# An id match in a DLRM look-up: one VectorE compare with row numbers in PSUM, or eight with all operands in SBUF

## What is computed

```python
e = jnp.stack([tbl_0[ids[:, 0]], ..., tbl_25[ids[:, 25]]], axis=1)
combined = jnp.concatenate([dense[:, None, :], e], axis=1)        # (2048, 27, 128)
inter = jnp.einsum('bnd,bmd->bnm', combined, combined)            # upper triangle is kept
h = jnp.concatenate([dense, inter_flat, dense], axis=1)
h = jnp.maximum(h @ W_top1 + b_top1, 0.0)
h = jnp.maximum(h @ W_top2 + b_top2, 0.0)
y = h @ W_top3
```

## Time and profile before

| | |
|---|---|
| median of 3 runs | 382.88 us (381.33 to 383.34) |
| profiled execution | 384.91 us |
| its span (first to last instruction) | 382.8 us |
| mean granted TensorE clock | 0.991 of full speed |
| POOL, 256 gathers | 248.8 us busy, 75.0 us of issue between them |
| DVE, 80 matches | 181.7 us busy |
| PE | 341.9 us busy |

### The profile page before, as it was taken

How to read it: one execution, slowest core, us unless ns; L and a number is a source line. 1 busy time by engine, 2 the same in 40 slices (tenths; PEclk the granted TensorE clock), 3 DMA queues, 4 the chain that set the end, 5 groups by cost and what they waited for, 6 DMA issues and landing times.

```text
span 382.8 us, 13108 instructions
## 1 busy us (share of the span) xinstructions
PE 341.9 (89%) x6048; PEld 304.2 (79%) x6048; DVE 193.2 (50%) x94; ACT 125.5 (33%) x211; POOL 252.1 (66%) x267
## 2 busy tenths in 40 slices
PE   0788878984999999999999999999999999999995
PEld 0687767883898898898988898889988898977763
DVE  2899996565424396228833495238742595100000
ACT  2235433332132341334322342323322333343122
POOL 3777887777777777777777777777777777500200
PEclk9999999999799999999999999999999999999999
DMA  8975698254322537225632536234622533420400
GB/s 205 222 210 166 170 301 250 58 195 126 126 80 58 193 82 200 58 80 177 149 119 58 194 92 190 58 120 140 187 79 58 193 89 86 144 73 27 154 13 0
DMA packets 30868, 49.57 MB, mean 129 GB/s; under 512 B 17499, under 2 KB 17635, under 8 KB 30686
## 3 DMA queue, kind: packets, MB, share of 16 engines
q1 hardware_dynamic: 22350, 31.68, 27.0%
q0 software_dynamic: 8320, 16.92, 16.8%
q10 hardware_dynamic: 144, 0.13, 0.1%
HBM read 38.21 MB, written 10.49 MB: 127 GB/s over the span
## 4 chain that ended last, share of the span: by engine, by line
PE 72%; POOL 14%; issue 6%; DMA 4%; DVE 2%; ACT 1%; DVEq 0%
PE look_ps L309 28%; POOL rows L290 14%; PE mid_ps L339 13%; PE layer_ps L356 11%; PE layer_ps L365 7%; PE mid_ps L321 7%; PE layer_ps L353 4%; DMA rows<-in_table,index 3%; DVE match L463 2%; PE layer_ps L372 2%; DMA index<-in_index 1%; ACT hidden L528 0%; ACT hidden L534 0%; ACT turned L501 0%; ACT turned L512 0%
## 5 line engine op out<-in xcount | busy, mean ns | idle before, releaser
L290 POOL DMA_INDIRECT rows<-in_table,index x256 | 248.8, 972 | 82.3 <-issue 75.0
L463 DVE TENSOR_TENSOR match<-look_ids,row_number_ps 125x2048 fp32r<-125x2048 int32 x80 | 181.7, 2286 | 132.2 <-PE look_ps L309 122.3
L309 PE MATMUL look_ps<-match,table_high 125*128 125x256 f32 x640 | 165.7, 296 | 20.2 <-DVE table_low L471 18.1
L309 PE MATMUL look_ps<-match,table_low 125*128 125x256 f32 x640 | 159.4, 286 | 0.1
L309 PEld LDWEIGHTS look_ps<-match,table_high 125*128 125x128 f32 x640 | 124.8, 195 | 25.0 <-issue 16.0
L309 PEld LDWEIGHTS look_ps<-match,table_low 125*128 125x128 f32 x640 | 125.1, 195 | 0.0
L339 PEld LDWEIGHTS mid_ps<-turned 128*32 128x32 f32 x4096 | 45.3, 109 | 19.1 <-issue 15.3
L339 PE MATMUL mid_ps<-turned 128*32 128x27 f32 x4096 | 54.4, 195 | 5.5 <-issue 1.7
L501 ACT COPY turned<-look_ps 128x512 f32<-128x512 f32 x40 | 31.9, 798 | 73.5 <-PE look_ps L309 72.2
L508 ACT COPY turned<-mid_ps 128x512 f32<-128x512 f32 x64 | 42.8, 672 | 19.7 <-PE mid_ps L321 19.5
L321 PE MATMUL mid_ps<-identity,rows 128*128 128x128 f32 x256 | 40.6, 283 | 9.4 <-DMA rows<-in_table,index 8.5
(11 more groups left out here) (21 smaller groups left out, 44.8 us busy)
## 6 DMA issues: line engine op xcount, KB each, us to landing
look_ids<-in_look_rows SPq DMA_DIRECT2D x40, 256.0 KB, 4.4
scratch<-grams SPq DMA_DIRECT2D x8, 864.0 KB, 4.4
rows<-in_table,index POOLq DMA_INDIRECT x256
scratch<-grams SPq DMA_DIRECT2D x8, 416.0 KB, 5.2
pairs<-scratch SPq DMA_DIRECT2D x92, 29.2 KB
grams<-in_table SPq DMA_DIRECT2D x4, 448.0 KB
pairs<-in_table SPq DMA_DIRECT2D x3, 448.0 KB
hidden<-in_table SPq DMA_DIRECT2D x3, 448.0 KB
```

Source lines behind the costliest of these rows:

```text
L290: pool.indirect_dma_start(out=rows[j % 2][:, at, :], out_offset=None, in_=tables[GATHERED[at]], in_offset=bass.IndirectOffsetOnAxis(ap=ind ...
L309: last = nc.tensor.matmul(look_ps[pair % 2][:, r % 2, :], part[0:table_rows, r, c, :], match[number % 2][0:table_rows, c, :], start=(c == ...
L463: nc.vector.tensor_tensor(match[number % 2][0:table_rows], look_ids[b][0:table_rows, r % 2].unsqueeze(1).broadcast_to(shape), row_number_p ...
```

## The change

The row numbers no longer go to PSUM but, as fp32, to a tile `row_number_f` in SBUF. The two rows of ids of a pair are cast to fp32 in place, once a pair, and DVE waits for its own cast. A match is then eight instructions, one per part c, each comparing the 256 ids of every partition with one row number per partition, `row_number_f[:, c:c+1]`. All operands of a match now lie in SBUF. The semaphore `match_ready` rises with the eighth compare, as it rose with the one before. The bank of PSUM that is freed is used for nothing.

```diff
+        row_number_f = sbuf("row_number_f", [P, PARTS])
...
-        row_number_ps = psum("row_number_ps", [P, PARTS])
-
...
+        ids_cast = sem("ids_cast")
...
+        def cast_number(g, q):
+            return pair_number(g, q)
...
                 b = pair % ID_SLOTS
+                ids_f = look_ids[b][0:table_rows].bitcast(fp32)
                 if r % 2 == 0:
                     dve.wait_ge(look_ids_in[b], 16 * (pair // ID_SLOTS + 1))
+                    nc.vector.tensor_copy(ids_f, look_ids[b][0:table_rows]).then_inc(ids_cast, 1)
+                    dve.wait_ge(ids_cast, cast_number(g, r // 2) + 1)
 
                 after(dve, look_done, number - 1)
-                shape = [table_rows, PARTS, N]
-                nc.vector.tensor_tensor(
-                    match[number % 2][0:table_rows],
-                    look_ids[b][0:table_rows, r % 2].unsqueeze(1).broadcast_to(shape),
-                    row_number_ps[0:table_rows].unsqueeze(2).broadcast_to(shape),
-                    ALU.is_equal).then_inc(match_ready, 1)
+                for c in range(PARTS):
+                    last = nc.vector.tensor_scalar(match[number % 2][0:table_rows, c, :], ids_f[:, r % 2, :],
+                                                   row_number_f[0:table_rows, c:c + 1], None, ALU.is_equal)
+                last.then_inc(match_ready, 1)
...
-            nc.vector.tensor_copy(row_number_ps[:], row_number[:]).then_inc(row_numbers_copied, 1)
+            nc.vector.tensor_copy(row_number_f[:], row_number[:]).then_inc(row_numbers_copied, 1)
```

## The result

The changed kernel is slower by 2.3%: 391.19 us median (388.16 to 393.56, 4 runs) against 383.11 us, a ratio of 1.0229 (95% interval 1.0172 to 1.0287). Run again in a later series it gave 392.94 us, ratio 1.0222 (1.0168 to 1.0277). The forecast was 456 us, with a range of 388 to 505. Medians and ranges are of all runs; the ratios leave out a run that is over 1.5% above the fastest of its kernel. The profiled execution took 388.16 us, the fastest of the four, with a span of 386.1 us; the one before was the slowest of its four (384.91 us, span 382.8). So the two profiles differ by 3.3 us, less than half of what the medians do.

What follows compares the result with a forecast made beforehand. It took POOL's gathers to bound the kernel up to 96 us, then PE, with POOL about 7 us behind. Gather holds of 77 us plus 3 for casts, less 7, gave +73 on 382.8: 456 us, range 388 to 505.

Steps and rivals of the forecast that it cites:

- What bounds the kernel: Whole kernel: gathers on POOL set the path up to 96.35 us, then PE, a group in some 42.4 us.
- The slack of 7 us: POOL at the run's end: it can lose about 7 us; any loss beyond comes out one for one.
- Step 1: Match on DVE: the new compare reads ids and row number from SBUF, so it can hold gathers; 80 matches of eight.
- the split's case: DVE instruction with two SBUF operands: a gather's index read waits for its end, then the gather needs 0.82 us.
- Step 2: Length of the eight compares on DVE: 1.58 us together, between 0.5 and 2.65, and 0.28 us for one.
- Step 3: Cast of the ids on DVE: 0.42 us, 40 times, lying in DVE's idle time except in the opening.
- Step 5: DVE's match: 1.8 us with half a cast against 2.2 before, taking off at most 0.7 us of PE's waiting.
- The last of the signs named in the prediction: DVE's compares: if POOL holds DVE instead, compares of up to 0.8 us stand among short ones.
- Step 6: POOL's gathers: each burst of eight holds one for 0.96 us, 77 us; with casts 80, less slack, +73 us.
- The let-in case: POOL's gathers: let in between compares, waiting 0.14 us on average; +10 us, 393 us in all; chance 0.27.
- the slow DVE: DVE's matches: no gather held, but one element a cycle, 2.65 us a match; 410 us in all; chance 0.07.
- The wholly stopped case: POOL's gathers: compares also stop descriptor writing, so gathers barely advance in bursts; up to +136, 519 us; chance 0.12.

Runs made afterwards that it cites:

- 32 gathers: Gathers stop after two tiles, 32 of 256, and later turns reread those rows: 368.33 us on the kernel before, 370.75 us on the changed kernel.
- the tail: The changed kernel with 27 more DVE instructions after its last match, compares and copies of 128, 256 and 512 elements: 387.21 us in its one run.

## Why the prediction was wrong

It was right that the change is slower, and wrong in size and in the engine that pays: +73 us on POOL was forecast, +8 us on DVE was measured. That 391 us lies inside the range of 388 to 505 is luck: its low end stood for POOL losing time to compares shorter than 0.28 us, and the compares took 0.34 us and POOL lost nothing.

**What bounds the kernel.** Right: with 32 gathers the kernel before falls from 382 to 368 us, and with gathers that are held (the second tensor in SBUF) the loss goes through to the end. The slack of 7 us fits the latter as well, the lower clock left aside: POOL loses 105 us and the kernel 99.

**Step 1, "the split's case, not the old match's".** This is the step that failed. It counted the row number as a second SBUF operand of the same kind as the split's. The run with the row number in PSUM shows that its place changes nothing, so it does not count as a second operand. The run with a second tensor in SBUF is the split's case: it held a gather in every match, for 1.4 us, where the changed kernel's bursts of eight hold one for 0.1 us or not at all. The compare is an instruction of one stream, at twice the rate of the DVE rows of before.

**Step 2, the length.** Forecast 0.28 us a compare, 1.58 the eight. Measured 0.34 and 2.18 with POOL idle, 2.51 in the mean beside the gathers. The rate that the Trainium skill gives ("VectorE: DVE Perf Modes", the perf-mode tier table), two elements a cycle, is about what the tail shows (141 ns for 256 more, half of what two tensors take). Too short was the fixed part: the bounds were built on the 0.146 us of a two-tensor instruction, and the compare has some 0.21, of which the value per partition is 0.06.

**Step 3, the cast.** Its size was right (0.42 forecast, 0.42 measured), "it lies in DVE's idle time except in the opening" was wrong. In the run of looks DVE has no idle time. Taking the cast away gives 6.4 us of median back, and 3.4 us with POOL idle.

**Step 5, DVE's own gain.** Forecast 1.8 us a match with its half of the cast. Measured, in the runs of looks: 2.53 to 2.65 from match to match, so DVE became the bound of the looks, which no term of the sum priced. The last of the signs named in the prediction, long compares among short ones, is what came.

**Step 6, POOL's loss.** Forecast 0.96 us a burst, 77 in all. Measured next to nothing: a gather loses 0 or 0.1 us to a burst, and POOL's total is 249.0 us after 248.8. This is the term that made the 73 us, and it rests on step 1: the burst does not act as one long instruction with two SBUF operands.

**The rivals.** The let-in case named 393 us, which is near, and its mechanism is there (17 of the 39 longer gathers lose 0.1 us each behind one compare), but it is not the cause: its time was to come out of POOL, and POOL's total did not change. The cause is nearest to the slow DVE, which had 7% and 410 us: the same wait of PE, but by a held instruction and a fixed part, not by one element a cycle. The wholly stopped case rested on the rule of the Trainium skill ("SBUF — State Buffer", Who interferes with whom) that whoever comes first has the shared pair for its whole instruction while the other blocks. The runs bear out that both can be the loser; here the held one ends 0.115 us after the other. They do not bear out "for the whole instruction" on POOL's side: compares in the middle of a gather run undisturbed.

## What to carry to other kernels

Where an engine has time to spare on average, look for the stretch in which its instructions follow one another at the pace of the bound: here DVE was busy for 58% of the span and still set the pace of four or five looks in most groups. Before breaking one instruction into eight to win a faster rate, price the start-to-start time of the new kind (0.262 us for 256 elements here), not its rate. And beside indirect gathers, a long DVE instruction with two tensors in SBUF is the form to avoid: it cost 26% here against the same compare with its row numbers in PSUM, which held no gather.

## What was not expected of the hardware

- A gather of 0.94 us holds a one-stream SBUF to SBUF instruction of DVE only near its end: the held one finishes 0.115 us after the gather. What the gather does there no run shows.
- A value per partition costs a compare 57 to 61 ns over a constant, at 128 elements (283 ns against 223) as at 512 (494 against 433).
- Four pieces of a two-tensor instruction in a row held a waiting gather to the end of the running piece in some cases (0.05 us) and to the end of the fourth in others (a gather of 1.98 us).
- The runs of the kernels with eight compares scatter more (390.3 to 396.7 us and 383.8 to 391.1) than those of the kernel before (380.4 to 385.4), and with them a longer time goes with a lower granted clock: without the cast, 383.77 us at 1.000 and 391.08 at 0.987. In the profile of the changed kernel run again, two groups at a granted clock of 0.96 take 46.5 us and their neighbours at 1.00 take 44.5. Why the clock falls in some runs and groups is not shown.
